# Gates, two layer norms and the output projection of a gated delta layer as one stage over tiles

## The reference

```python
out = dplr_delta_rule(q, k, v, a, gk).reshape(b, n, d)
gate = jax.nn.sigmoid(x @ Wg1 @ Wg2)
out = out * gate
out = (out - mu) * jax.lax.rsqrt(var + 1e-05) * norm_w
h = h + out @ Wo
x = _layernorm(h)
w_t = jnp.clip(jnp.round(w / jnp.mean(jnp.abs(w))), -1.0, 1.0)   # W1 and W2
```

## Time and profile before

| | us |
|---|---|
| median of 3 runs | 1865.17 (1865.06 to 1865.77) |
| profiled execution, its own time | 1864.77 |
| span of the profiled execution | 1863.0 |
| first matmul of "gates" | 1694.80 |
| first matmul of `ternary_ffn` | 1782.85 |

### The profile page before, as it was taken

One profiled execution on the slowest core, in us unless ns is written; L12 is line 12 of the kernel. 1 busy time (PEld: TensorE's weight loads), 2 busy tenths in 40 slices (PEclk: granted clock), 3 DMA queues, 4 the chain that ended last, 5 costly groups with the idle time before them and its releaser, 6 DMA issues. The chain is left out here.

```text
span 1863.0 us, 51134 instructions
## 1 busy us (share of the span) xinstructions
PE 1668.8 (90%) x22625; PEld 1486.2 (80%) x22625; DVE 1107.2 (59%) x2382; ACT 658.8 (35%) x1362; POOL 341.8 (18%) x305
## 2 busy tenths in 40 slices
PE   8899978999999999999999999676898988766699
PEld 8787756998889999999999999465777877666468
DVE  7677757545554555555465555646664556545885
ACT  6466634222222223322232222344333333322142
POOL 4633344000000000000000000343322322200630
PEclk9899979999999999999999999777666676655689
DMA  6000011000010000001010000100000000001001
GB/s 209 1 2 3 2 49 46 1 23 23 3 44 1 24 23 24 24 1 46 1 46 1 1 1 1 38 2 2 4 4 4 4 4 3 4 4 50 0 12 43
DMA packets 11709, 36.23 MB, mean 19 GB/s; under 512 B 3400, under 2 KB 8032, under 8 KB 8928
## 3 DMA queue, kind: packets, MB, share of 16 engines
q1 hardware_dynamic: 11488, 32.97, 5.1%
HBM read 30.47 MB, written 2.49 MB: 18 GB/s over the span
## 5 line engine op out<-in xcount | busy, mean ns | idle before, releaser
L1126 ACT ACTIVATE hidden<-bank,moe_b 128x512 f32<-128x512 f32 (+1 forms) x320 | 213.6, 669 | 536.5 <-PE bank L1018 523.8
L1035 PE MATMUL bank<-moe_w2h,hidden_hi 128*128 128x256 f32 x1216 | 345.7, 284 | 0.0
L1035 PE MATMUL bank<-moe_w2l,hidden_hi 128*128 128x256 f32 x1216 | 344.0, 283 | 0.0
L1035 PE MATMUL bank<-moe_w2h,hidden_lo 128*128 128x256 f32 x1216 | 344.0, 283 | 0.0
L1018 PE MATMUL bank<-x_hi,moe_w1h 128*128 128x512 f32 (+1 forms) x640 | 243.7, 381 | 2.9 <-ACT hidden L1126 2.8
L1160 DVE SCALAR_TENSOR_TENSOR residual<-bank,gates,residual 128x256 f32<-128x256 f32 x152 | 73.4, 484 | 290.3 <-PE bank L1035 290.3
L1018 PE MATMUL bank<-x_lo,moe_w1h 128*128 128x512 f32 (+1 forms) x640 | 242.5, 379 | 0.0
L1018 PE MATMUL bank<-x_hi,moe_w1l 128*128 128x512 f32 (+1 forms) x640 | 242.0, 378 | 0.0
L1035 PEld LDWEIGHTS bank<-moe_w2h,hidden_hi 128*128 128x128 f32 x1216 | 233.1, 192 | 6.0 <-DVE residual L1160 4.3
L1035 PEld LDWEIGHTS bank<-moe_w2l,hidden_hi 128*128 128x128 f32 x1216 | 233.2, 192 | 1.2
L1035 PEld LDWEIGHTS bank<-moe_w2h,hidden_lo 128*128 128x128 f32 x1216 | 233.2, 192 | 0.0
(11 more groups left out here) (297 smaller groups left out, 3258.3 us busy)
## 6 DMA issues: line engine op xcount, KB each, us to landing
moe_w<-in_moe_w SPq DMA_DIRECT2D x16, 1024.0 KB, 4.9
patches<-in_patches SPq DMA_DIRECT2D x7, 864.0 KB, 6.9
out<-residual SPq DMA_DIRECT2D x19, 128.0 KB, 1.7
ffn_w<-in_ffn_w SPq DMA_DIRECT2D x2, 1024.0 KB, 5.8
att_w<-in_att_w SPq DMA_DIRECT2D x1, 1536.0 KB, 10.4
delta_w<-in_delta_w SPq DMA_DIRECT2D x1, 1280.0 KB
patches<-in_patches SPq DMA_DIRECT2D x6, 144.0 KB, 3.2
tok_w<-in_tok_w SPq DMA_DIRECT2D x6, 128.0 KB, 2.6
```

The source lines that it names most:

```text
L1035: mm = nc.tensor.matmul(bank[4 + n % 3][:, 0:D], left, right, start=(i == 0), stop=(i == len(passes) - 1))
L1126: nc.scalar.activation(H[:, i % 4, 0:n], bank[i % 4][:, 0:n], ACT.Relu, bias=b1[:, x, f:f + 1]).then_inc(acted, 1)
```

## The change

The four stages become one, `output_tail`. The first nine tiles (`LEAD`) of gates, token rows, product and statistics come first; then DVE sums the weights, and a loop of steps j = 0, 1, ... runs all parts, each on a tile of its own: at step j PE turns gated tile j, makes the token rows of tile j + 9, projects tile j - 1 and turns the sum of tile j - 3. Both norms are now applied by ACT, as `Identity` with a scale and a bias per token, where the bias (minus the mean times the inverse deviation) is made by DVE in a `scalar_tensor_tensor`. The deviations of the first norm are taken in three groups (tiles 0 to 8, 9 to 13, 14 to 18), those of the second tile by tile. POOL makes the ternary weights in 16 pieces of 256 columns, three instructions each. Each use of PSUM has two banks.

```diff
-            with stage(nc, "o_tile", "g_tile", "gate_ready", ...
...
-            layer_norm_turn(nc, bank, Y, STD, MV, XN, XH, XL, ident, "lno", pool_work=ternary(0))
-            add_product_and_stats(nc, bank, RES, BN, MV, XH, XL, wh[:, O], wl[:, O], "delta_o", pool_work=ternary(1))
-        layer_norm_turn(nc, bank, RES, STD, MV, XN, XH, XL, ident, "ln3")
+            output_tail(nc, bank, ins, RES, BN, MV, STD, XN, XH, XL, ident, identr, G1, wg2s, wh[:, O], wl[:, O],
+                        w1, w2, b1, b2, up, down, ones, S, flat, tern, Y, SG, shift, eps)
+LEAD = 9
+PARTS = HALVES * FF // D
+GROUPS = (range(0, LEAD), range(LEAD, 14), range(14, TILES))
...
+        @block.tensor
+        def _(pe):
...
+            def turn_gated(t):
+                pe.wait_ge(normed_1, t + 1)
+                if t >= 2:
+                    pe.wait_ge(lo_1, t - 1)
...
+            def project(t):
+                pe.wait_ge(lo_1, t + 1)
+                if t == 1:
+                    pe.wait_ge(scaled, 1)
+                if t >= 2:
+                    pe.wait_ge(summed, t - 1)
...
+            def turn_sum(t):
+                pe.wait_ge(normed_2, t + 1)
+                if t < 2:
+                    pe.wait_ge(gate_ready, TILES)
+                else:
+                    pe.wait_ge(lo_2, t - 1)
...
+            for t in range(LEAD):
+                gate(2 * t)
+                gate(2 * t + 1)
+                token_rows(t)
+            gate(2 * LEAD)
+            pe.wait_ge(abs_sum, 2)
+            pe.wait_ge(ones_set, 1)
+            nc.tensor.matmul(bank[7][:, 0:2], ones[:, :], S[:, 0, :], start=True, stop=True).then_inc(total, 1)
+            for j in range(TILES + 3):
+                if j < TILES:
+                    turn_gated(j)
+                token_rows(j + LEAD)
+                if 0 <= j - 1 < TILES:
+                    project(j - 1)
+                if 0 <= j - 3 < TILES:
+                    turn_sum(j - 3)
...
+        @block.scalar
+        def _(act):
...
+            def norm_gated(t):
+                act.wait_ge(shift_1, group(t) + 1)
+                if t >= 2:
+                    act.wait_ge(turned_1, t - 1)
+                nc.scalar.activation(XN[:, t % 2, :], Y[:, t, :], ACT.Identity, bias=shift[:, 0, t:t + 1],
+                                     scale=STD[:, 2, t:t + 1]).then_inc(normed_1, 1)
...
+            def deviation(t):
+                act.wait_ge(mv_2, t + 1)
+                nc.scalar.activation(STD[:, 0, t:t + 1], MV[:, t, 1:2], ACT.Sqrt, bias=eps[:, 0:1]).then_inc(std_2, 1)
...
+            for t in range(TILES):
+                act.wait_ge(g_ready, t + 1)
+                nc.scalar.activation(SG[:, t, :], bank[2 + t % 2][:, 0:D], ACT.Sigmoid).then_inc(gate_ready, 1)
+            act.wait_ge(eps_set, 1)
+            deviations(0)
+            norm_gated(0)
+            for j in range(TILES + 3):
+                if 0 <= j - 3 < TILES:
+                    deviation(j - 3)
+                if j < TILES:
+                    high_gated(j)
+                if j in (6, 11):
+                    deviations(1 if j == 6 else 2)
+                if j + 1 < TILES:
+                    norm_gated(j + 1)
+                if 0 <= j - 3 < TILES:
+                    norm_sum(j - 3)
+                    high_sum(j - 3)
...
+        @block.vector
+        def _(dve):
...
+            def inverse(t):
+                dve.wait_ge(std_2, t + 1)
+                nc.vector.reciprocal(STD[:, 0, t:t + 1], STD[:, 0, t:t + 1]).then_inc(inv_2, 1)
+                dve.wait_ge(inv_2, t + 1)
+                nc.vector.scalar_tensor_tensor(out=shift[:, 1, t:t + 1], in0=MV[:, t, 0:1], scalar=-1.0,
+                                               in1=STD[:, 0, t:t + 1], op0=ALU.mult, op1=ALU.mult).then_inc(shift_2, 1)
...
+            dve.wait_ge(loaded, 64)
+            for i in range(2):
+                nc.vector.tensor_reduce(S[:, 0, i:i + 1], flat[i], AX.X, ALU.add,
+                                        apply_absolute_value=True).then_inc(abs_sum, 1)
+            inverses(0)
+            dve.wait_ge(total, 1)
...
+            for j in range(TILES + 5):
+                if 0 <= j - 1 < TILES:
+                    low_gated(j - 1)
+                if 0 <= j - 3 < TILES:
+                    inverse(j - 3)
+                gated(j + LEAD)
+                if 0 <= j - 4 < TILES:
+                    low_sum(j - 4)
+                if 0 <= j - 2 < TILES:
+                    add(j - 2)
+                gated_stats(j + LEAD)
+                if 0 <= j - 2 < TILES:
+                    sum_stats(j - 2)
+                gated_aggregate(j + LEAD)
+                if 0 <= j - 2 < TILES:
+                    sum_aggregate(j - 2)
+                if j in (6, 11):
+                    inverses(1 if j == 6 else 2)
...
+        @block.gpsimd
+        def _(pool):
+            pool.wait_ge(cut, 2)
+            for i in range(2):
+                for q in range(PARTS):
+                    n, qs = i * PARTS + q, slice(q * D, (q + 1) * D)
...
+                    nc.gpsimd.tensor_scalar(up[:, qs], flat[i][:, qs], S[:, 2, i:i + 1], None, ALU.is_gt).then_inc(ups, 1)
...
```

More of the change, by code:

```diff
@@ L1374, in last_layer @@
             Y = sb(own, "gated_out", [P, TILES, D])
[L1375 to L1423, removed]
-                        if t == TILES:
-                            dve.wait_ge(total, 1)
-                            nc.vector.tensor_scalar(S[:, 1, :], bank[6][:, 0:2], 1.0 / (D * FF), 1e-8,
-                                                    ALU.mult, ALU.max).then_inc(step, 1)
-                            dve.wait_ge(step, 4)
-                            nc.vector.tensor_scalar(S[:, 2, :], S[:, 1, :], 0.5, None, ALU.mult).then_inc(step, 1)
-                            nc.vector.tensor_scalar(S[:, 3, :], S[:, 1, :], -0.5, None, ALU.mult).then_inc(step, 1)
-                        if t < TILES:
-                            dve.wait_ge(o_ready, t + 1)
-                            dve.wait_ge(gate_ready, t + 1)
-                            nc.vector.tensor_tensor(Y[:, t, :], bank[t % 4][:, 0:D], SG[:, t % 4, :],
-                                                    ALU.mult).then_inc(y_ready, 1)
-                        if 1 <= t <= TILES:
-                            dve.wait_ge(y_ready, t)
-                            nc.vector.bn_stats(BN[:, t - 1, :], Y[:, t - 1, :]).then_inc(bn_ready, 1)
-                        if t >= 2:
-                            dve.wait_ge(bn_ready, t - 1)
-                            nc.vector.bn_aggr(MV[:, t - 2, :], BN[:, t - 2, :]).then_inc(mv_ready, 1)
@@ L1444, in ternary @@
-            def ternary(i):
-                def work(pool, done):
-                    nc.gpsimd.tensor_scalar(up[:], flat[i], S[:, 2, i:i + 1], None, ALU.is_gt).then_inc(done, 1)
-                    nc.gpsimd.tensor_scalar(down[:], flat[i], S[:, 3, i:i + 1], None, ALU.is_lt).then_inc(done, 1)
-                    pool.wait_ge(done, 2)
-                    nc.gpsimd.tensor_tensor(tern[i], up[:], down[:], ALU.subtract).then_inc(done, 1)
-                return work
-            layer_norm_turn(nc, bank, Y, STD, MV, XN, XH, XL, ident, "lno", pool_work=ternary(0))
@@ L1454, in last_layer @@
-            add_product_and_stats(nc, bank, RES, BN, MV, XH, XL, wh[:, O], wl[:, O], "delta_o", pool_work=ternary(1))
-        layer_norm_turn(nc, bank, RES, STD, MV, XN, XH, XL, ident, "ln3")
-        ternary_ffn(nc, sb, bank, RES, XH, XL, out, w1t, w2t, b1, b2)
+            SG = sb(own, "gate", [P, TILES, D])
+            shift = sb(own, "minus_mean", [P, 2, TILES])
+            eps = sb(own, "tail_eps", [P, 1])
+            output_tail(nc, bank, ins, RES, BN, MV, STD, XN, XH, XL, ident, identr, G1, wg2s, wh[:, O], wl[:, O],
+                        w1, w2, b1, b2, up, down, ones, S, flat, tern, Y, SG, shift, eps)
```

134 lines of the change are left out of this document (added).

## The result

The changed kernel took 1853.99 us (median of 5 runs, 1844.19 to 1857.16) against 1865.17 for the kernel before, 11.2 us less by these medians. The recorded ratio, which uses every run of both kernels, is 0.9926, 95% interval 0.99 to 0.9953, so 13.8 us less (8.8 to 18.7). Run again unchanged (a_again) it gave 0.9932 (0.9913 to 0.995), 12.7 us. The forecast had the sign and the range, and less than half of the size (6.5 us).

What follows compares the result with a forecast made beforehand. Each of four stages had its own limit, with three barriers between. The new stage's terms put ternary_ffn's first matmul at 1776.3 instead of 1782.85: 1864.77 - 6.5 = 1858.3, with the median 0.4 above; predicted 1858.5, range 1852 to 1865.

Steps and rivals of the forecast that it cites:

- ACT's closed chain: In the loop ACT's next deviation stands behind its last high part: 2.65 us a step, deciding steps 10 to 18.
- steps 3 to 9: Loop steps with everything in them: PE longest at 3.0 us, taken as 3.05 with hops, 21.4 us in all.
- steps 10 to 18: Loop steps without token rows, product or first statistics: ACT's loop of 2.65 us decides, 23.9 us in all.
- with the clock at 0.50 as the default: PE's clock through the new stage, taken as 0.50 because three of the four old stages have it.
- rival (a): Projections raise the clock in the new stage and it stays: 5.8 us more gain, near 1853; chance 0.27.
- Half a piece is 0.34: DVE's scalar_tensor_tensor in the loop waits half a POOL piece of 0.68 us, making DVE's step 2.95 us.
- Rival (c): POOL's hold of the shared port delays a second DVE instruction each step: slower, 1869 to 1872 us; chance 0.06.
- ACT's normalisation: One normalisation on ACT in the loop: 0.60 us, bounds 0.46 and 0.64, against 0.40 on DVE.
- Rival (d): Identity and Sqrt need different tables, two loads a step on ACT: 49 us slower, near 1907; chance 0.03.
- The 12.7 us of waiting: In the old stage lno, DVE waits some 12.7 us on POOL's instructions; these go but are not the gain.
- Rival (b): No gain: in-order engines' waits add 0.2 to 0.5 us in 16 middle steps, 1861.5 to 1866.5; chance 0.16.
- POOL, costed at nothing: POOL's 48 instructions, 31 us in all from 1714.5, end before the loop even with half as much again.

Runs made afterwards that it cites:

- f_no_tern: Changed kernel with the ternary weights left out, POOL only copying raw weights before the loop; ratio 0.9925 to the kernel before, rewritten stretch 74.3 us.
- g_dve_norm: Changed kernel with both normalisations put back on DVE as tensor_scalar; ratio 0.9964 to the kernel before, rewritten stretch 82.5 us.
- c_act: Kernel before, four stages and whole POOL instructions, with stages lno and ln3 normalising on ACT; ratio 0.9973, rewritten stretch 80.7 us against 88.05.
- k_turns: Changed kernel with the sum's high part on ACT, low part on DVE and turn on PE each one step later; ratio 0.9911, rewritten stretch 73.8 us.
- d_whole: Changed kernel with POOL's ternary weights in 2 pieces of 2048 columns instead of 16 of 256; ratio 0.9999, rewritten stretch 87.0 us.
- m_no_tensor_tensor: Changed kernel with POOL's third instruction of each piece a tensor_scalar comparison instead of a tensor_tensor; ratio 0.9917, rewritten stretch 73.8 us.

## Why the prediction was right and wrong

The mechanism was right but for the clock. ACT's closed chain was named for the later steps, the port's small instruction was found, and the sign followed; the early steps were given to PE, with DVE close behind, and DVE alone decided them. Wrong was the size. By the prediction's own terms, for the profiled execution of the changed kernel:

| term | predicted | measured | error |
|---|---|---|---|
| start to the first deviation of the second norm | 27.3 | 26.5 | -0.8 |
| steps 3 to 9 | 21.4 | 19.6 | -1.8 |
| steps 10 to 18 | 23.9 | 22.6 | -1.3 |
| two later groups of deviations | 0.7 | in the steps | -0.7 |
| steps 19 to 21 | 7.3 | 6.95 | -0.35 |
| low part and barrier | 1.0 | 1.2 | +0.2 |
| tail | 81.6 | 76.9 | -4.7 |

**The step that failed** is "with the clock at 0.50 as the default", and with it "Steps 3 to 9 ... The longest is 3.0". The clock came up to 1.00 at 1710.9 (in a_again at 1723.0), as the projections filled the loop; PE's 3.0 us a step fell away and DVE's sum stood there alone. The 3.0 were right for the low clock: in a_again, before the clock rose, PE ran the 12 matmuls of step 2 from 1720.38 to 1722.94 without a pause, 2.56 us or 0.213 each, 3.0 for 14. DVE's sum was right too: 2.61 without the port, measured 2.60 in f_no_tern. With the port the steps are 2.60 to 3.29 long, 2.80 on average. This was my rival (a), at 0.27 against 0.48, and the prediction itself had named a clock of 1.00 through the loop as a sign of being wrong. That its time of 1853 is so nearly the one that came is in part luck: by its terms the tail would be 75.7 us, and it was 76.9. I had weighed "in 'gates' it was busy 21.2 of 25.8 us at 0.50" over the window of "delta_o", the only row with projections, at 0.87. The nearer row was among those that I quoted. What the clock is worth at the chain can be read inside a_again, in one step at each level:

```profile
1758.27:1760.96 2.69, 1.74 (x10) 1.23 (x10) 2.48 (x8) 1.93 (x7) 1.08 (x2) 0.92 0.00 0
1760.96:1763.61 2.65, 2.48 (x12) 2.38 (x12) 2.11 (x8) 1.81 (x7) 0.00 (x0) 0.50 0.00 0
```

The second, at 0.50 and without GpSimd beside it, is 2.65 us long, to the hundredth the chain that I had summed at the low clock; the same chain at 1.00 is 2.34 (f_no_tern). The first is that long at a high clock because of the port: its `scalar_tensor_tensor` lasted 0.73. The two lengths of the turn, from the changed kernel's timeline, are the 0.53 and 0.78 in brackets:

```profile
1718.77 0.38 ACT L1522 ACTIVATE x_hi<-bank 128x256 fp32r<-128x256 f32 x1 [0.53 <-PE bank L1470]
...
1759.77 0.38 ACT L1522 ACTIVATE x_hi<-bank 128x256 fp32r<-128x256 f32 x1 [0.78 <-PE bank L1470]
```

No run here holds the clock down for a whole loop, so the whole price of this error is only read from such steps: some 0.3 for each of 9 late ones, 2.8 us, of which the port and the few steps at 0.50 took 1.6 back.

**The port** at "Half a piece is 0.34" was twice too dear: 0.18 a step in steps 3 to 9. The pieces are longer than I had them (0.93, 0.93 and 0.73 for 5.47 / 8 = 0.68 and 4.50 / 8 = 0.56), but the wait is shorter, for the reason in the last section. What the prediction didn't see is that the loop falls into step with GpSimd: a piece takes it 2.69 us, and while the small instruction starts in every step beside a `tensor_tensor` and ends with it, the step takes 2.69 or 2.70 us too, be it 2.60 or 2.34 by itself (last section). Rival (c), a second instruction held, didn't happen: the low parts of the loop average 0.39 and 0.41 us.

**ACT's normalisation** at 0.60 was right (0.593 and 0.596), and so was the choice against the rule that I weighed. The Trainium skill ("ScalarE: Activation LUTs", Rules for kernel authors) would have multiplications and additions on VectorE. For the instruction the trace agrees (0.40 us on DVE); for the kernel g_dve_norm decides against it, by 0.55 us a step where I had said 0.5. Rival (d), two tables for `Identity` and `Sqrt`, is refuted: between the first deviation and the end of the loop ACT loads no table. The Trainium skill ("ScalarE: Activation LUTs", Table sets: the hidden batching unit) says that identity is in every set, and the trace agrees.

**The 12.7 us of waiting.** The prediction said that they "are thus not the gain: they go ... but the loop costs what four stages had in turn". The experiments put it more sharply. They can be had without the loop: c_act alone has 7.3 of the 11.3 us, with POOL in whole matrices. Pieces alone, pieces and ACT, or the loop without pieces bring 1.8, 1.2 and 1.1 us, and the whole runs of none of the three can be told from those of the kernel before. The loop is what lets POOL's longer, divided work lie beside everything, and the pieces are what lets the loop live beside POOL; each is worth 10 us, but only given the other.

**Rival (b)**, hops and waits of in-order queues, didn't show in steps 3 to 9 (DVE 97% busy). POOL, costed at nothing, ended at 1747.0 (43.3 us instead of the 31 of the sum, within the half more that was allowed for), 14 us ahead of the end. The head was 13.6 us for 14.3: a step of it took PE 1.28 us and not 1.38.

## What to carry to other kernels

Take an unknown clock from the window whose instructions resemble the new stage most, and give its other level a chance of its own: here, in this one case, the choice moved a 3.0 us step to 2.6. Ask of two edits whether each needs the other before adding what they bring: cutting work into pieces costs its engine more time, and pays only if nothing waits for the last piece. In a loop over in-order engines, follow a stall after you have removed it: the wait that left ACT's queue by one reordering was in PE's queue until that was reordered as well, and only both together brought the 2.34 us chain to 2.06. And before a gain of 1 or 2 us is given to an edit, compare the granted clock step by step: between two of these traces it was worth up to 1.1 us, and the place of GpSimd's pieces beside the small instruction 1.2.

## What the runs showed of the hardware

DVE's small `scalar_tensor_tensor` with both inputs in SBUF waits for GpSimd by kind of instruction. Timeline of a_again:

```profile
1746.03 0.93 POOL L1652 TENSOR_SCALAR is_up<-ffn_w,scales 128x256 f32<-128x256 f32 x1
1746.27 0.24 DVE L1595 SCALAR_TENSOR_TENSOR minus_mean<-mean_var,std 128x1 f32<-128x1 f32 x1
...
1748.71 0.93 POOL L1652 TENSOR_SCALAR is_up<-ffn_w,scales 128x256 f32<-128x256 f32 x1
1748.80 0.40 DVE L1595 SCALAR_TENSOR_TENSOR minus_mean<-mean_var,std 128x1 f32<-128x1 f32 x1
...
1756.07 0.74 POOL L1657 TENSOR_TENSOR w_ternary<-is_up,is_down 128x256 fp32r<-128x256 f32 x1
1756.09 0.73 DVE L1595 SCALAR_TENSOR_TENSOR minus_mean<-mean_var,std 128x1 f32<-128x1 f32 x1
...
1758.76 0.74 POOL L1657 TENSOR_TENSOR w_ternary<-is_up,is_down 128x256 fp32r<-128x256 f32 x1
1758.79 0.73 DVE L1595 SCALAR_TENSOR_TENSOR minus_mean<-mean_var,std 128x1 f32<-128x1 f32 x1
```

The last four rows are the falling into step: 1756.07 and 1758.76 on POOL are 2.69 us apart, 1756.09 and 1758.79 on DVE 2.70, where the same steps take 2.34 in f_no_tern. In k_turns the loop gets out of it: its small instruction started 0.05 us ahead of a `tensor_tensor` (1750.54 and 1750.59) and took 0.16.

Beside a `tensor_tensor` it ends with it: 0.75 us after its start (0.74 to 0.76 in all eight cases of a_again, 4.54 in d_whole). Beside a `tensor_scalar` of 0.93 us it ends 0.48 us after that one's start if it began 0.07 to 0.3 after it, and is free (0.16) when it began 0.32 or more after the start, or within 0.05 of it (k_turns has the 0.05, at 1756.72). The delay and the length add up to 0.48 or 0.49 each time: 0.24 + 0.24 and 0.09 + 0.40 in the rows above, 0.23 + 0.25 and 0.18 + 0.30 in m_no_tensor_tensor. For 2048 columns it was let go 3.7 us into 5.44 (d_whole, three times). The Trainium skill ("SBUF — State Buffer", its rule on the shared port pair) has the later of the two blocked for the whole instruction of the other: the trace agrees for the `tensor_tensor`, and for the `tensor_scalar` the measurement differs. A `tensor_scalar` of DVE waited for the end of GpSimd's in the kernel before, yet in g_dve_norm cost only 0.03 to 0.09 over 0.40 on average; why, no run here shows.

Cutting GpSimd's instructions has a fixed price: 0.93 us for 256 columns and 5.44 for 2048 make 0.29 each beside 2.5 ns a column; for the `tensor_tensor` (0.73 and 4.51) it is 0.19 beside 2.1. And 128x512 parts of the sum on DVE cost 0.65 us each, where the whole 128x2048 cost 2.2.
